# Two graph layers on a 4096-node adjacency: `adj` read in runs of 1 KB, eight groups of 32 rows a tile, from the second chunk on in two rounds of four tiles

## The chip, the cores and the metric

The kernel runs on one core of one Trainium2 chip. The metric is device time in microseconds. The kernel before took 587.05 us (median of 3 runs, 586.03 to 588.43).

## What is computed

Two graph layers over the same dense 4096 x 4096 float32 matrix `adj`. Shortened from the reference:

```
h  = relu(layernorm(x))
m  = mobius_matvec(weight, h); m = mobius_add(m, exp(bias)); x_tangent = logmap0(m)
support_t = adj @ x_tangent                      # 4096 x 4096 times 4096 x 128
x  = x + proj(expmap0(relu(logmap0(proj(expmap0(support_t))))))
h2 = relu(layernorm(x))
left, right = (context @ W_common.T) @ w_left + b_left, ... @ w_right + b_right
logits = leaky_relu(left[:, None] + right[None, :]), minus infinity where adj <= 0
x  = x + relu(softmax(logits) @ h2)
```

So `adj` (64 MB) is used once as numbers, in `adj @ x_tangent`, and once as a mask of edges, in the softmax.

## The kernel before

**Phase 1** reads `adj` once. TensorE contracts over partitions, so each piece of `adj` must be turned: nodes that are columns of `adj` have to lie on partitions. The 4096 rows are cut into 8 chunks of 512 rows (`NC = 8`, `CH = 512`), a chunk into 8 tiles of 512 columns (1 MB each), and a tile into 4 units, which the code calls blocks (`k`, 32 a chunk, `NK = 32`). `loaded` holds 4 tiles (`XSLOTS`), `turned` 4 units (`TSLOTS`). A tile comes in four loads of 256 KB, one for each 32 partitions (`b`): partitions 0 to 63 (`LOW`) are loaded by SP's queue, 64 to 127 (`HIGH`) by ACT's queue; the first four tiles all by SP's, and after them SP's queue brings `context` in 16 loads. A partition receives 16 runs of 128 floats, 512 B, from rows that lie 32 rows apart (line 281).

For each unit the engines do this, each in the order of its own program, coupled by semaphores:

- SP (line 360) waits until the last unit of a tile that held the slot is turned, then issues the slot's next two loads (line 362).
- DVE (`turn_block`, line 955) waits at a tile's first unit for its four loads (`adj_in`), at each unit for the product that used the `turned` slot (`block_multiplied`) and at every second for ACT's Sign (`half_signed`), and transposes 32 x 32 squares of a 128 x 512 piece (line 964).
- PE (`product`, line 678) multiplies `xt[:, k]` (128 x 128, float32) with the turned 128 x 512 piece and accumulates over the 32 units of the chunk into one of two banks, `acc[parity]` (line 686). Each float32 product stands in the profile as two records.
- ACT (`signs`, line 821) writes for each two units the sign of 1024 elements a partition into `mask`, int8, all of which stays in SBUF (line 836), and after every second Sign issues the two `HIGH` loads of the tile whose slot has come free (`load_high`, line 731). An issue that is held up holds up what ACT does after it.

After a chunk, ACT copies its sums (line 794, the first Sign of the next chunk stands before it), PE turns them (`turn_support`), and DVE, ACT and POOL do the norms and the residual beside the next chunk; POOL stores and loads rows of `x` (lines 561, 568).

In chunk 0, the tangent vectors `xt` are made on the fly: ACT makes a bias part for each of 32 blocks (`bias_part`, line 780, four ahead, then two after each Sign) and DVE makes a tangent from it (`tangent`, line 1081), one after each unit. PE's product of unit k waits for tangent k (`xt_ready`).

**Phase 2** (from about 325 us on) works from `mask` alone: comparisons, bit operations and products in fp8 and float16 (line 712). The order of nodes within a chunk is free as long as `x`, `context`, `out` and `adj` agree on it; lines 277 and 280 set it for the first three.

## Time and profile before

| | |
|---|---|
| median of 3 runs | 587.05 us (586.03 to 588.43) |
| span of the profiled execution | 587.9 us; no separate time of that one execution is given, and its span lies inside the three runs |
| instructions | 8561 |
| PE busy | 493.0 us, 84% |
| DVE busy | 448.0 us, 76% |
| ACT busy | 312.3 us, 53% |
| POOL busy | 268.5 us, 46% |
| DMA | 157445 packets, 84.72 MB, 144 GB/s over the span |

The span is one execution from the first to the last instruction. Busy shares are averages over two phases with different limits, so the page's 40 slices (of 14.7 us) come first, and then windows cut where a chunk ends. In "idle before" a number says how long an engine did nothing and what ended it. ACTq and SPq are the issuing of loads on these two queues; PEld is the weight load that belongs to a matmul.

### The profile page before, as it was taken

What the parts mean: (1) busy time and instruction counts of PE and PEld (TensorE: products, weight loads), DVE (VectorE), ACT (ScalarE), POOL (GpSimd) and SP (SyncE); (2) the same over time, 40 slices, a digit from 0 to 9 for tenths busy, and PEclk for the clock granted to TensorE, in tenths of its full rate; (3) what the DMA queues carried; (4) which work ended last, traced back from release to release, by engine and by line L of the source; (5) the groups of instructions that cost most, each with busy time, mean ns of one, the idle gap of its engine ahead of it and who ended that gap; (6) DMA issues with size and microseconds to landing.
All of it is one profiled execution on the core that took longest, in us unless ns stands there. A gap on an engine that the chain in (4) does not pass through costs nothing.

```text
span 587.9 us, 8561 instructions
## 1 busy us (share of the span) xinstructions
PE 493.0 (84%) x2695; PEld 309.4 (53%) x2695; DVE 448.0 (76%) x923; ACT 312.3 (53%) x466; POOL 268.5 (46%) x333
## 2 busy tenths in 40 slices
PE   2625999987989888888789457789999999999995
PEld 1522444332433332333333245668888888888884
DVE  4998987867767666656576999996969696969773
ACT  1666977655757556464465663243545444454521
POOL 5930057979696886917243799420202020111100
PEclk9976999999999999999899698989999999999998
DMA  7999999999999999999996010101010101011010
GB/s 161 218 222 213 233 287 284 288 265 266 247 274 277 236 258 240 251 234 228 216 250 146 19 37 1 37 18 37 19 37 21 37 19 37 19 37 37 1 37 18
DMA packets 157445, 84.72 MB, mean 144 GB/s; under 512 B 7600, under 2 KB 155312, under 8 KB 157408
## 3 DMA queue, kind: packets, MB, share of 16 engines
q1 hardware_dynamic: 89760, 47.60, 38.1%
q10 hardware_dynamic: 65232, 32.25, 26.2%
q0 software_dynamic: 2416, 4.41, 2.8%
q8 instruction: 19, 0.31, 0.2%
q14 instruction: 18, 0.15, 0.1%
HBM read 80.02 MB, written 4.21 MB: 143 GB/s over the span
## 4 chain that ended last, share of the span: by engine, by line
PE 36%; DMA 28%; DVE 20%; ACT 6%; issue 4%; ACTq 3%; POOL 2%; SPq 0%; DVEq 0%; POOLq 0%
PE ps L712 33%; DMA room<-in_adj_dram 27%; DVE room L964 5%; ACT mask L836 4%; PE ps L686 3%; ACTq L731 3%; DVE room L1199 2%; DVE room L1150 1%; DVE room L1166 1%; DVE mask L923 1%; DVE stats L1110 1%; DVE mask L976 1%; DVE room L1173 1%; DVE mask L972 1%; DMA mask<-in_x_dram 1%
## 5 line engine op out<-in xcount | busy, mean ns | idle before, releaser
L686 PE MATMUL ps<-room 128*128 128x512 f32 x512 | 241.5, 614 | 46.5 <-DVE room L964 29.0
L712 PE MATMUL ps<-room 128*128 128x258 f16 x2048 | 232.0, 276 | 23.2 <-POOL room L601 16.2
L712 PEld LDWEIGHTS ps<-room 128*128 128x128 fp8e4 x2048 | 200.4, 98 | 54.8 <-issue 16.9
L964 DVE STREAM_TRANSPOSE room<-room 128x512 f32<-128x512 f32 x256 | 167.0, 689 | 79.2 <-DMA room<-in_adj_dram 70.4
L836 ACT ACTIVATE mask<-room,constants 128x1024 int8<-128x1024 f32 x128 | 144.4, 1143 | 101.4 <-DVE room L964 92.9
L686 PEld LDWEIGHTS ps<-room 128*128 128x128 f32 x512 | 91.7, 192 | 190.8 <-DVE room L964 134.8
L615 POOL TENSOR_TENSOR h_room<-h_room 128x512 f32<-128x512 f32 x7 | 8.9, 1273 | 148.0 <-DVE post L1240 148.0
L1166 DVE SCALAR_TENSOR_TENSOR room<-mask,constants,room 128x512 int32<-128x512 int32 x64 | 62.2, 972 | 7.6 <-ACT room L885 7.6
L885 ACT ACTIVATE room<-relu_u,r_col 128x512 int8<-128x512 f32 x64 | 42.0, 713 | 42.3 <-PE ps L712 42.3
L885 ACT ACTIVATE room<-room,r_col 128x512 int8<-128x512 f32 x62 | 40.9, 712 | 34.1 <-PE ps L712 34.1
L464 POOL TENSOR_TENSOR mask<-mask,h_room 128x2048 f32<-128x2048 f32 x8 | 36.3, 4536 | 45.4 <-DVE room L1081 45.2
L1173 DVE SCALAR_TENSOR_TENSOR room<-mask,constants,room 128x512 int32<-128x512 int32 x64 | 47.6, 744 | 0.3
L473 POOL TENSOR_TENSOR mask<-mask 128x1024 f32<-128x1024 f32 (+6 forms) x56 | 44.9, 801 | 4.0
L1150 DVE TENSOR_SCALAR room<-room,r_col 128x512 int8<-128x512 f32 x66 | 37.6, 613 | 9.3 <-PE ps L712 9.3
L906 ACT ACTIVATE h_room<-ps,factors 128x258 f32<-128x258 f32 x32 | 15.2, 477 | 50.0 <-PE ps L712 49.0
L1150 DVE TENSOR_SCALAR room<-relu_u,r_col 128x512 int8<-128x512 f32 x64 | 32.2, 544 | 11.5 <-PE ps L712 11.5
L1229 DVE SCALAR_TENSOR_TENSOR h_room<-ps,factors,h_room 128x258 f32<-128x258 f32 x32 | 15.3, 485 | 16.8 <-ACT h_room L906 16.1
L568 POOL DMA_DIRECT2D xk<-in_x_dram x32 | 18.0, 569 | 19.4 <-ACT h_room L814 18.5
L532 POOL TENSOR_TENSOR post<-post,powers 128x8 f32<-128x8 f32 x8 | 13.5, 1686 | 24.6 <-DVE post L1104 24.6
L561 POOL DMA_DIRECT2D out_dram<-xk x32 | 18.3, 577 | 2.4 <-POOL xk L546 2.4
L1199 DVE SCALAR_TENSOR_TENSOR room<-h_room,factors,room 128x128 f16<-128x128 f32 x32 | 18.5, 639 | 0.0
L814 ACT ACTIVATE h_room<-xk,post 128x128 f32<-128x128 f32 x32 | 13.1, 479 | 9.8 <-POOL post L554 9.8
(158 smaller groups left out, 333.2 us busy)
## 6 DMA issues: line engine op xcount, KB each, us to landing
room<-in_adj_dram SPq DMA_DIRECT2D x136, 256.0 KB, 9.0
room<-in_adj_dram ACTq DMA_DIRECT2D x120, 256.0 KB, 10.9
mask<-in_L_gnn_context_dram SPq DMA_DIRECT2D x16, 256.0 KB, 10.8
xk<-in_x_dram POOLq DMA_DIRECT2D x32, 64.0 KB, 7.0
out_dram<-xk POOLq DMA_DIRECT2D x32, 64.0 KB, 6.5
h_room<-out_dram SPq DMA_DIRECT2D x32, 64.0 KB, 2.5
out_dram<-h_room SPq DMA_DIRECT2D x28, 64.0 KB, 1.7
mask<-in_x_dram SPq DMA_DIRECT2D x22, 64.0 KB, 4.2
```

The lines of the kernel that those rows point to most:

```text
L464: side(tt(room_of, cx[:, ks, :], v_rows[:, w, :].unsqueeze(1).broadcast_to([P, BESIDE, C]), ALU.mult))
L473: side(tt(dst, room_of[:, :, 0:n], room_of[:, :, n:2 * n], ALU.add))
L561: pool.dma_start(out_n[p, b], xk[b * Q:(b + 1) * Q]).then_inc(x1_stored, 16)
L686: pe.matmul(acc[parity], xt[:, k, :], turned[:, k % TSLOTS, :], start=(k == 0), stop=(k == NK - 1)).then_inc(block_multiplied, 1)
L712: mm = pe.matmul(ps[:, 2 * t + w, 0:GW], part[slot(c, g)][:, kk, t * P:(t + 1) * P], G[w][:, k, :], start=(k == 0), stop=(k == NK - 1))
L836: nc.scalar.activation(mc[:, half * HB:(half + 1) * HB, :], turned[:, slots:slots + HB, :], ACT.Sign, bias=constants[:, 4:5], scale=EDGE_S ...
L885: ins = nc.scalar.activation(signs_of[slot(c, g)][:, kk, :], nl[parity], ACT.Sign, scale=-1.0, bias=r_col[:, k:k + 1])
L964: v.transpose(turned[:, k % TSLOTS, :].rearrange("p (l b i) -> p b l i", l=L, b=NQ), loaded[:, g % XSLOTS, :, l * Q:(l + 1) * Q].rearrange ...
L1150: ins = v.tensor_scalar(signs_of[slot(c, g)][:, kk, :], nl[parity], r_col[:, k:k + 1], -1.0, ALU.is_gt, ALU.mult)
L1166: v.scalar_tensor_tensor(out=neg_words[n], in0=edges_of(c, g), scalar=ones, in1=neg_words[n], op0=ALU.bitwise_and, op1=ALU.bitwise_and).th ...
L1173: v.scalar_tensor_tensor(out=pos_words[n], in0=edges_of(c, g), scalar=ones, in1=neg_words[n], op0=ALU.bitwise_and, op1=ALU.bitwise_xor).th ...
L1199: v.scalar_tensor_tensor(out=G[1][:, k, D:2 * D], in0=h2[:, k, :], scalar=s1_col[:, k:k + 1], in1=G[1][:, k, 0:D], op0=ALU.mult, op1=ALU.s ...
```

## The change

Three things change together, and the names `W = 256` and `RH = 8` carry them.

1. **The shape of a tile.** A tile is now 256 rows by 1024 columns, the same 1 MB, still four loads of 256 KB for 32 partitions each. A partition receives 8 runs of 256 floats, 1 KB, from rows that lie 256 rows apart: eight groups of 32 rows a tile. A load has 256 runs where it had 512. The order of the nodes follows: a chunk's rows are eight groups of 32 rows in each half of the matrix, and `x`, `context` and `out` are addressed in the same order (`(l b s q)` for `(s b l q)`), still in runs of 512 B, 1 KB and 512 B.
2. **What a unit is.** A turned unit still is 128 x 512 elements, now two blocks of 128 columns of `adj` for 256 rows. PE makes two products with 256 columns each, with two blocks of `xt`, where it made one with 512; the sums of a chunk lie in the first 256 columns of two banks. ACT's Sign writes the same 1024 elements in four stretches of 256, the copy of the sums reads two stretches of 256.
3. **The order of tiles.** In chunk 0 the two row halves of a column group follow each other, so that half of the tiles need no new block of `xt`: DVE makes two tangents after each unit of an even tile and none in an odd one. From chunk 1 on the four column groups come for the first 256 rows and then for the next 256.

Late in phase 1 DVE waits for 24 instead of 16 products of the last chunk before it writes comparisons over `xt`.

```diff
+W = L * NQ * 16
+RH = L * NQ // 2
-        loaded = view(room, o, [XSLOTS, L * NQ, L * Q], F32)
+        loaded = view(room, o, [XSLOTS, RH, W], F32)
-        acc = [ps[:, 0, :], ps[:, 1, :]]
+        acc = [ps[:, 2 * n:2 * n + 2, 0:CH // 2] for n in (0, 1)]
-            return t.rearrange("(s b l q) d -> s b q l d", b=NQ, l=L, q=Q)
+            return t.rearrange("(l b s q) d -> s b q l d", b=NQ, l=L, q=Q)
-        cx_l = context.rearrange("(s b l q) d -> l b q s d", b=NQ, l=L, q=Q)
-        adj_n = adj.rearrange("(s r p) (g b j) -> s g b p r j", r=CH // Q, p=Q, b=NQ, j=L * Q)
+        cx_l = context.rearrange("(l b s q) d -> l b q s d", b=NQ, l=L, q=Q)
+        adj_n = adj.rearrange("(h r s q) (l b j) -> s l h b q r j", h=2, r=RH, q=Q, b=NQ, j=W)
+        def load_tile(eng, c, tile, quarters):
+            for b in quarters:
+                eng.dma_start(loaded[b * Q:(b + 1) * Q, tile % XSLOTS],
+                              adj_n[c, *run_and_half(c, tile), b]).then_inc(adj_in[tile % XSLOTS], 16)
+        def run_and_half(c, tile):
+            return (tile // 2, tile % 2) if isinstance(c, int) and c == 0 else (tile % L, tile // L)
+        def blocks_of(c, unit):
+            first = unit % L * 2 * L + run_and_half(c, unit // L)[0]
+            return first, first + L
+        tangent_order = [k for unit in range(NK) if unit // L % 2 == 0 for k in blocks_of(0, unit)]
...
                     if number and c == 0:
-                        pe.wait_ge(xt_ready, k + 1)
-                    pe.matmul(acc[parity], xt[:, k, :], turned[:, k % TSLOTS, :],
-                              start=(k == 0), stop=(k == NK - 1)).then_inc(block_multiplied, 1)
+                        pe.wait_ge(xt_ready, tangent_order.index(blocks_of(c, k)[1]) + 1)
+                    l, h = run_and_half(c, k // L)
+                    for j in range(2):
+                        mm = pe.matmul(acc[parity][:, h], xt[:, tangent_order.index(blocks_of(c, k)[j]), :],
+                                       turned[:, k % TSLOTS, j * (CH // 2):(j + 1) * (CH // 2)],
+                                       start=(l == 0 and k % L == 0 and j == 0),
+                                       stop=(l == L - 1 and k % L == L - 1 and j == 1))
+                    mm.then_inc(block_multiplied, 1)
...
-                    nc.scalar.activation(mc[:, half * HB:(half + 1) * HB, :], turned[:, slots:slots + HB, :],
+                    (l, h), s = run_and_half(c, half // HALVES), half % HALVES * L
+                    nc.scalar.activation(mc[:, l, h, s:s + L],
+                                         turned[:, slots:slots + HB, :].rearrange("p s (j i) -> p (s j) i", j=2),
                                          ACT.Sign, bias=constants[:, 4:5], scale=EDGE_SCALE).then_inc(
...
-                    turned[:, k % TSLOTS, :].rearrange("p (l b i) -> p b l i", l=L, b=NQ),
-                    loaded[:, g % XSLOTS, :, l * Q:(l + 1) * Q].rearrange("p (b l) q -> p b l q", b=NQ)).then_inc(
+                    turned[:, k % TSLOTS, :].rearrange("p (j r i) -> p j r i", j=2, r=RH),
+                    loaded[:, g % XSLOTS, :, 2 * l * Q:2 * (l + 1) * Q].rearrange("p r (j q) -> p j r q", j=2)).then_inc(
...
-                    if number and c == 0:
-                        tangent(k)
+                    if number and c == 0 and k // L % 2 == 0:
+                        for k_ in blocks_of(c, k):
+                            tangent(tangent_order.index(k_))
...
-            dve.wait_ge(block_multiplied, (NC - 1) * NK + NK // 2)
+            dve.wait_ge(block_multiplied, (NC - 1) * NK + NK - 2 * L)
```

How instructions stand in a row, DVE in chunk 0, units 8 to 12 (the transposes are line 964, the tangents 1081; in the changed kernel 985 and 1103). Before:

```order
L964 STREAM_TRANSPOSE room<-room 128x4x4x32 [waits half_signed,block_multiplied,adj_loaded_2]
L1081 SCALAR_TENSOR_TENSOR room<-mask 128x128 [waits fb_ready]
L964 STREAM_TRANSPOSE room<-room 128x4x4x32 [waits block_multiplied]
L1081 SCALAR_TENSOR_TENSOR room<-mask 128x128 [waits fb_ready]
L964 STREAM_TRANSPOSE room<-room 128x4x4x32 [waits half_signed,block_multiplied]
L1081 SCALAR_TENSOR_TENSOR room<-mask 128x128 [waits fb_ready]
L964 STREAM_TRANSPOSE room<-room 128x4x4x32 [waits block_multiplied]
L1081 SCALAR_TENSOR_TENSOR room<-mask 128x128 [waits fb_ready]
L964 STREAM_TRANSPOSE room<-room 128x4x4x32 [waits half_signed,block_multiplied,adj_loaded_3]
```

and now, from unit 7 to unit 13:

```order
L985 STREAM_TRANSPOSE room<-room 128x512 [waits block_multiplied]
L985 STREAM_TRANSPOSE room<-room 128x512 [waits half_signed,block_multiplied,adj_loaded_2]
L1103 SCALAR_TENSOR_TENSOR room<-mask 128x128 [waits fb_ready] x2
L985 STREAM_TRANSPOSE room<-room 128x512 [waits block_multiplied]
L1103 SCALAR_TENSOR_TENSOR room<-mask 128x128 [waits fb_ready] x2
L985 STREAM_TRANSPOSE room<-room 128x512 [waits half_signed,block_multiplied]
L1103 SCALAR_TENSOR_TENSOR room<-mask 128x128 [waits fb_ready] x2
L985 STREAM_TRANSPOSE room<-room 128x512 [waits block_multiplied]
L1103 SCALAR_TENSOR_TENSOR room<-mask 128x128 [waits fb_ready] x2
L985 STREAM_TRANSPOSE room<-room 128x512 [waits half_signed,block_multiplied,adj_loaded_3]
L985 STREAM_TRANSPOSE room<-room 128x512 [waits block_multiplied]
```

The tangents of units 12 to 15 have moved ahead, two behind each transpose of units 8 to 11, and from unit 12 on transposes follow each other directly.

ACT in chunk 0, units 4 to 7 (Sign, bias parts, the two loads of a tile's upper half). Before:

```order
L836 ACTIVATE mask<-room,constants 128x1024 [waits block_turned]
L780 ACTIVATE mask<-mask 128x128 [waits xt_ready] x2
L836 ACTIVATE mask<-room,constants 128x1024 [waits block_turned]
L780 ACTIVATE mask<-mask 128x128 [waits xt_ready] x2
L731 DMA room<-in_adj_dram 32x16x128 x2
```

and now:

```order
L856 ACTIVATE mask<-room,constants 128x4x256 [waits block_turned]
L798 ACTIVATE mask<-mask 128x128 [waits xt_ready] x2
L856 ACTIVATE mask<-room,constants 128x4x256 [waits block_turned]
L798 ACTIVATE mask<-mask 128x128 [waits xt_ready] x2
L288 DMA room<-in_adj_dram 32x8x256 x2
```

Nothing has moved here; the same two bias parts stand behind each Sign, and a load has 8 runs of 256 for each of 32 partitions instead of 16 of 128.

PE in chunks 0 and 1 (the products of `adj`, and `turn_support` between them). Before:

```order
L666 MATMUL ps<-mask 128x256 x2
L686 MATMUL ps<-room 128x512 x35
L675 MATMUL ps<-ident,room 128x128 x4
L686 MATMUL ps<-room 128x512 x29
```

and now:

```order
L683 MATMUL ps<-mask 128x256 x2
L705 MATMUL ps<-room 128x256 x70
L692 MATMUL ps<-ident,room 128x128 x4
L705 MATMUL ps<-room 128x256 x58
```

Each product of 512 columns has become two of 256; `turn_support` stands behind the same unit.

## Rows read from the trace of the kernel before

**Rows 1.** The page: 40 slices, busy tenths, granted clock, DMA, GB/s.

```profile
PE   2625999987989888888789457789999999999995
...
DMA  7999999999999999999996010101010101011010
GB/s 161 218 222 213 233 287 284 288 265 266 247 274 277 236 258 240 251 234 228 216 250 146 19 37 1 37 18 37 19 37 21 37 19 37 19 37 37 1 37 18
```

**Rows 2.** Windows: us, busy (x) of PE, PEld, DVE, ACT, POOL; PEclk, DMA, GB/s.

```profile
50.40:82.26 31.86, 31.79 (x69) 13.64 (x70) 27.67 (x63) 27.39 (x47) 2.64 (x1) 0.94 1.20 242
82.26:112.29 30.03, 29.17 (x68) 11.69 (x67) 23.79 (x46) 20.72 (x22) 25.78 (x28) 1.00 1.20 291
112.29:146.88 34.59, 29.70 (x68) 11.59 (x67) 25.42 (x46) 20.88 (x26) 29.73 (x36) 1.00 1.20 265
146.88:179.57 32.69, 30.57 (x71) 12.13 (x70) 24.02 (x47) 20.84 (x25) 26.78 (x37) 1.00 1.20 265
179.57:215.60 36.03, 30.94 (x71) 11.51 (x69) 24.17 (x46) 20.87 (x26) 28.71 (x30) 1.00 1.20 254
215.60:251.63 36.03, 31.36 (x70) 11.45 (x68) 23.36 (x46) 20.82 (x25) 26.32 (x39) 1.00 1.21 245
251.63:292.31 40.68, 31.28 (x67) 12.04 (x67) 23.83 (x49) 20.87 (x26) 15.40 (x27) 0.96 1.17 226
292.31:324.45 32.14, 29.21 (x65) 10.61 (x63) 22.09 (x46) 20.23 (x26) 14.24 (x28) 1.00 0.92 193
```

**Rows 3.** Chain of waits by line, 82 to 246, then 246 to 325 us.

```profile
by line: DMA room<-in_adj_dram 71.6%; DVE room L964 13.3%; ACT mask L836 3.8%; issue 3.5%; DVE stats L1110 2.0%; PE ps L686 2.0%; DVE post L1103 1.8%; DVE post L1099 1.8%; DVE post L1119 0.6%; DVE mv L1117 0.6%; ACTq L731 0.6%; DVE post L11
...
by line: DMA room<-in_adj_dram 37.2%; ACTq L731 19.4%; ACT mask L836 19.1%; PE ps L686 10.2%; DVE room L964 5.1%; issue 4.0%; ACT h_room L814 2.6%; DVE stats L1110 1.3%; ACT ps L801 0.6%; ACT ps L800 0.6%; DVE mv L1117 0.4%; DVE post L1119 
```

**Rows 4.** Who waited for line 362 (SP); line 731 (ACT): ns min/median/max, waits.

```profile
  DVE room L964: 1.1, 1
...
L731 ACTq DMA_DIRECT2D room<-in_adj_dram x120: 317/1768/5837, 51.1 to 307.3; - x120
...
  DVE room L964: 69.3, 48
```

**Rows 5.** DMA, one queue alone: 20 to 29, then 42 to 49 us.

```profile
DMA packets 3986, 1.99 MB, mean 221 GB/s; under 512 B 118, under 2 KB 3985, under 8 KB 3985
...
room<-in_adj_dram SPq DMA_DIRECT2D x8, 256.0 KB, 7.4
...
DMA packets 1582, 1.53 MB, mean 218 GB/s; under 512 B 92, under 2 KB 1582, under 8 KB 1582
...
mask<-in_L_gnn_context_dram SPq DMA_DIRECT2D x4, 256.0 KB, 10.8
```

**Rows 6.** DMA, both queues: 80 to 96, then 190 to 206 us.

```profile
DMA packets 9227, 4.62 MB, mean 289 GB/s; under 512 B 273, under 2 KB 9224, under 8 KB 9224
...
DMA packets 7260, 3.81 MB, mean 238 GB/s; under 512 B 283, under 2 KB 7195, under 8 KB 7259
```

**Rows 7.** Timeline of ACT, 283 to 294 us: an idle stretch for an issue.

```profile
282.94 1.15 ACT L836 ACTIVATE mask<-room,constants 128x1024 int8<-128x1024 f32 x1 [5.88 <-issue]
```

**Rows 8.** Groups of PE and PEld by form, and PE's timeline at 109 us.

```profile
L666 PE MATMUL ps<-mask 128*128 128x256 f32 x4 | 1.1, 405 | 0.0
...
L666 PEld LDWEIGHTS ps<-mask 128*128 128x128 f32 x4 | 0.7, 189 | 0.1
...
109.62 3.70 PE L686 MATMUL ps<-room 128*128 128x512 f32 x8 [0.55 <-DVE room L964]
113.16 0.60 PE L675 MATMUL ps<-ident,room 128*128 128x128 f32 x4
```

**Rows 9.** Timelines of ACT and of DVE in chunk 0.

```profile
53.27 0.68 ACT L780 ACTIVATE mask<-mask 128x128 f32<-128x128 f32 x2
...
59.33 0.31 DVE L1081 SCALAR_TENSOR_TENSOR room<-mask 128x128 f32<-128x128 f32 x1
59.56 0.70 DVE L964 STREAM_TRANSPOSE room<-room 128x512 f32<-128x512 f32 x1
```

More of the change, by code:

```diff
@@ L839, in signs @@
                     if number and c == 0:
[L840 to L841 removed]
+                        for n in range(XT_AHEAD + half * HB, min(NK, XT_AHEAD + (half + 1) * HB)):
+                            bias_part(n)
                     if half in steps:
```

40 lines of the change are left out of this document (18 added, 22 removed).

## The prediction

> **What bounds the kernel now.** I read the slices first. DMA stands at 9 tenths from slice 2 to slice 21, PE at 7 to 9 only from slice 5 on, and the moved GB/s are not constant: 284 to 288 in slices 6 to 8, 216 to 250 in slices 19 to 21 [rows 1]. So the first phase, up to about 325 us, is the part that loads `adj`, and the change touches nothing else of weight. Then I cut it at the eight copies of a finished chunk on ACT (line 794): the chunk passes take 31.9, 30.0, 34.6, 32.7, 36.0, 36.0, 40.7 and 32.1 us [rows 2]. The first two are PE's own pace, since PE is busy 31.79 of 31.86 and 29.17 of 30.03 us. In the later six PE idles 2 to 9 us a pass, and the loads run at 265 falling to 193 GB/s. The chain of waits says the same: from 82 to 246 us 71.6% of it is loads of `adj`; from 246 to 325 us it is 37.2% loads, 19.4% the issuing of loads on ACT's queue (line 731) and 19.1% ACT's Sign [rows 3]. And of the 70.4 us that DVE waits for tiles, 69.3 us are for loads that ACT issued, 1.1 us for SP's [rows 4]. ACT's issues have a median of 1.77 us and a longest of 5.84 us, where an unblocked one takes 0.32 us [rows 4], so the queue pushes back.
>
> What the queue pushes back with shows in the bytes. With one queue alone, packets of mostly 512 B ran at 221 GB/s and packets of mostly 1 KB (`context`) at 218 GB/s: 16 engines x 9 us / 3986 = 36.1 ns a packet of 499 B, and 16 x 7 / 1582 = 70.8 ns one of 967 B [rows 5]. There, time goes by bytes. With both queues level, 512 B packets reach 289 GB/s (16 x 16 us / 9227 = 27.7 ns each); later, with the same packets and the same two queues, 238 GB/s [rows 6].
>
> **The change part by part.** *Packets of 1 KB.* 131072 packets of 512 B become 65536 of 1 KB, same bytes. The lower bound of the gain is nothing, from the single-queue rows [rows 5]. The upper bound: if the part that goes by bytes is halved when both queues feed (36.1 / 2 = 18 ns) and the other 9.7 ns of the 27.7 are per packet, 1 KB takes 36 + 10 = 46 ns, or 356 GB/s, 20% over 289. The four passes from 112 to 252 us run at 245 to 265 GB/s, between both states, so I take the middle, 10%: 139.3 us (34.59 + 32.69 + 36.03 + 36.03) / 1.1 = 126.7, a gain of 12.7 us [rows 2]. The second pass is PE's: 32 blocks of 0.86 us and a turn_support of 0.60 us [rows 8] are about 28.5 us with the two handovers, so at most 1.5 us, and I take 0.9.
>
> *Issues.* With half the descriptors a queue holds more bytes before it pushes back: when SP went from loads of 512 descriptors to loads of 256 of the same 256 KB, the median from issue to landing went from 7.4 to 10.8 us at an unchanged 218 to 221 GB/s [rows 5]. So more lies queued, and ACT should issue in 0.3 to 0.5 us instead of 1.77. The pass of 40.68 us holds the longest idle stretch of ACT for an issue, 5.88 us [rows 7]. I let it fall to its neighbours' 36.03 / 1.1 = 32.8: 7.9 us. The last pass has PE idle 2.9 of 32.1 us; half of it, 1.5 us.
>
> *Matmuls.* A block's one product with 512 columns (two records of 0.43 us) becomes two with 256 columns, each with its own weights (eight records of 512 columns took 3.70 us). The nearest row has exactly the new shape: four records of 128x256 f32 in 1.1 us, 405 ns each with their overlap, so (1.1 - 0.4) / 3 = 0.23 us apart at most, the first one's longer start in it; the weight load lasts 0.19 us [rows 8]. Half of 0.43 is 0.215 us, and four such records are 0.86 us as before. I take 0; the bound above is 0.23 us a record, 0.06 us a block, 2 us a pass, which would fall on the passes that PE bounds. What hides a weight load is the preceding product of 0.215 us: it has 0.02 us to spare.
>
> *Transposes, signs, copies.* DVE's transposes read and write the same 128x512 (0.70 us), ACT's Sign the same 1024 elements (1.15 us), the copy the same 512 [rows 7, 9]. Only strides change. Either could rise by some tenths unseen: DVE is busy about 24 of 33 us a pass, ACT 21 [rows 2], so 0.1 us on each of 32 transposes would be covered. I take 0 for each, with bounds 0 and 1 us a pass.
>
> *Tangents.* In chunk 0 they come two with each unit of an even tile. ACT still makes two bias parts per Sign. In tiles 2, 4 and 6 the last pair must wait for the Sign of its own unit: a transpose 0.70, Sign 1.15, two bias parts 0.68, two tangents 0.54 (0.31, and 0.23 between two starts), so 3.1 us before PE has that block, where a block costs PE 0.86 [rows 7, 9]. Two units of such a tile wait; I get 10 us for a pair of tiles instead of 8 x 0.86 = 6.9, so up to 9 us for three pairs. Behind it on DVE stands the next transpose, and for that PE, ACT's Sign, and both queues' next loads, since a slot comes free later. Below, it costs nothing if loads bound the chunk anyway: four slots are a run-ahead of some 16 us of loading, and later passes wait for loads. I take 3 us.
>
> *The second phase.* DVE's wait for 24 instead of 16 blocks of the last chunk stands behind a transpose that needs 28, so it costs nothing. The loads of `x` and rows of `out` keep their 512 B.
>
> The sum, against the span of 587.9 us (the three timed runs have 586.0 to 588.4, median 587.05, so no correction): 587.9 - 12.7 - 0.9 - 7.9 - 1.5 + 3 = 567.9, and I say **568 us**.
>
> **A rule against the change.** In the rows above, eight groups of 32 rows a tile stand 32 rows x 16 KB = 512 KB apart before, and `context`'s runs too; no row shows a wider pitch. Afterwards the groups are 256 rows, 4 MB, apart. The Trainium skill, "DMA: Bandwidth & Descriptors", section "Latency and other measured facts", reports half the rate for a pitch of 4 MiB against one of 512 KiB (103 and 207 GB/s), where the streams of the partitions run in lockstep at that pitch. Here the 32 partitions of one load stay 16 KB apart and only an engine's successive packets lie 4 MB apart, so I hold it less likely than not; no run here shows it yet.
>
> A second rule explains the two rates: "SBUF — State Buffer", section "Door 1: The DMA port swizzle", says that partitions 0 to 63 reach only eight of 16 ports and gives 27.2 GB/s a port, 218 for eight. The rows agree (218 to 221 with one queue). By it packet size brings nothing whenever one queue leads.
>
> **The rivals.**
> *PE becomes the bound everywhere.* For: packets were fast once the queues were level, 291 GB/s in the second pass, and only 8.9 MB a pass are needed, 312 GB/s at PE's 28.5 us. Then 82.3 + 3 + 7 x 28.5 = 284.8 where 324.4 stands: 39.6 less, 548 us; with the whole 9 us of tangents 554. Against: it needs 7% more than the best stretch, sustained.
> *Bytes, not packets.* The rate stays as it is and only ACT's stall goes, which the tangents eat: 587.9 - 0 to 5 + 3, about 588 us. For: rows 5. Against: rows 6, where 512 B packets take 27.7 ns.
> *The wider stride slows the loads.* Mechanism: successive packets of an engine, 4 MB apart, meet the same part of the memory and queue there. Place: every load of `adj`. From 82 to 324 us 59.9 MB are moved, on average 247 GB/s; that is the point from which it decides. At the 220 GB/s of rows 5 it is 272 us instead of 242: 588 + 30 + 3 = 621 us; at 240 GB/s, 599.
> *Tangents uncovered with no gain in rate*: 587.9 + 9 - 1.5 = 595 us.
>
> **How the numbers follow.** Forecast as summed (556 to 582): 0.45. PE as the bound (546 to 556): 0.20. Bytes (584 to 590): 0.12. Wider stride: 0.15. Tangents alone: 0.08. A change of 0.5% is about what a measurement of this kernel can tell from none. So faster 0.65, same 0.12, slower 0.23. The range of 8 in 10 runs from the PE bound to the mild form of the stride: 547 to 600; it leaves the severe stride and the lower edge outside.
>
> **What would show it.** DMA slices should read 265 GB/s or more from 82 us on with about 65,000 fewer packets; the median of ACT's issues of `adj` below 1 us; DVE's wait for loads well under 70 us; PE's records twice as many with the same total of busy time; passes 3 to 7 of about 31 us; the first pass 3 to 9 us longer, with DVE or PE waiting on bias parts. I am wrong if the GB/s of passes 2 to 6 are at or below 247, if weight loads leave PE idle between two products of a block, or if the passes stay long while DMA drops below 9 tenths.

## The result and the profile after

The changed kernel takes 572.51 us (median of four runs, 570.08 to 573.64); the kernel before takes 587.74 us beside it (four runs, 586.03 to 589.52). The ratio is 0.9725, with a 95% interval of 0.9679 to 0.9771. The forecast was 568 us in a range of 547 to 600. A second series, on another chip, gave 573.08 us (571.16 to 574.06) for the changed kernel and 583.1 us for the kernel before (median of eleven runs, 578.32 to 600.02), with a ratio of 0.9853 (0.9789 to 0.9917). So the changed kernel repeats its time within 0.6 us, the kernel before does not, and the gain is 15.2 us in the first series and 8 to 10 us in the second. (All ratios leave out executions that fell in the chip's slower state; of one experiment below, the kernel before with an addition moved, that leaves one of four, so it carries no verdict.)

The profiled run of after took 573.64 us with a span of 571.8 us against 587.9, so 16.1 us have to be placed. No trace shows a run of before near 580 us; how much of each difference below is such scatter of before, and how much the change, is not shown.

The first phase can be cut at the same eight copies of a finished chunk as in [rows 2]; they are at line 812 now. The view is the windows of after, with the columns of [rows 2]: us, busy time (and instructions) of PE, PEld, DVE, ACT, POOL; PE's granted clock, DMA share, GB/s.

```profile
50.70:90.32 39.62, 33.93 (x130) 27.49 (x131) 28.70 (x62) 26.97 (x45) 5.85 (x2) 0.88 0.95 211
90.32:120.25 29.93, 29.30 (x138) 25.50 (x137) 26.49 (x47) 21.05 (x22) 22.20 (x26) 1.00 1.08 282
120.25:153.04 32.79, 28.41 (x128) 24.41 (x128) 27.96 (x47) 21.23 (x25) 30.11 (x37) 0.94 0.96 276
153.04:184.22 31.18, 30.70 (x138) 26.44 (x137) 26.44 (x47) 21.31 (x26) 24.45 (x30) 0.96 1.02 282
184.22:217.46 33.24, 28.86 (x128) 24.24 (x128) 27.74 (x47) 21.09 (x26) 30.06 (x37) 0.94 0.96 273
217.46:248.86 31.40, 30.91 (x138) 26.59 (x137) 26.45 (x47) 21.31 (x26) 24.45 (x30) 0.95 1.03 282
248.86:280.64 31.78, 28.59 (x131) 24.75 (x131) 24.68 (x49) 21.20 (x25) 17.91 (x35) 0.97 1.10 257
280.64:310.94 30.30, 28.67 (x130) 24.07 (x128) 23.19 (x49) 20.12 (x26) 14.66 (x29) 0.98 0.84 226
310.94:571.84 260.90, 231.70 (x2052) 200.44 (x2052) 211.55 (x362) 114.99 (x209) 70.84 (x64) 0.97 0.10 26
```

Against [rows 2], pass by pass: the first is 7.8 us longer (39.62 for 31.86) and starts 0.3 us later. The second is level (29.93 for 30.03). The third to sixth take 128.6 us for 139.3, which is 10.7 less. The seventh takes 31.78 for 40.68, 8.9 less, the eighth 30.30 for 32.14, 1.8 less. What follows the last copy takes 260.9 us; before it took 587.9 - 324.45 = 263.4, so 2.5 less. 8.1 - 0.1 - 10.7 - 8.9 - 1.8 - 2.5 = -15.9, which is the difference of the spans but for rounding. The change does not touch the second phase. 260.8 us stand there in several experiments too, and 261.0 in another trace of the kernel before (the experiment with its addition moved), so the profile of before was a little long in that part; I have no cause for it.

The page of after, the lines that answer to [rows 1], and its count of packets:

```profile
PE   1724879999699979999697648799999999999995
...
DMA  7999899999799998999893010101111010101010
GB/s 165 201 230 226 198 226 233 281 285 324 221 268 305 292 311 199 299 284 300 221 286 91 21 37 1 38 20 38 22 36 29 29 32 25 39 18 38 1 38 18
DMA packets 91911, 84.75 MB, mean 148 GB/s; under 512 B 7600, under 2 KB 89776, under 8 KB 91872
```

There are 65,534 packets fewer than the 157,445 of before. The rate is no longer falling from pass to pass: 282, 276, 282, 273, 282 GB/s stand where [rows 2] had 291, 265, 265, 254, 245. But DMA drops to 7 or 8 tenths every few slices, and PE's digit falls to 6 or 7 in the same slice or beside it. So something other than loads now interrupts the work. Who waits is told by the line that issues the loads (288), which answers to [rows 4]. Columns: ns min/median/max, first and last start; then who waited for the loads, us and times.

```profile
L288 SPq DMA_DIRECT2D room<-in_adj_dram x136: 311/452/1414, 13.8 to 296.0; - x136
L288 ACTq DMA_DIRECT2D room<-in_adj_dram x120: 318/415/1735, 51.1 to 296.1; - x120
...
  DVE room L985: 12.0, 10
```

ACT's issues have a median of 0.415 us instead of 1.768 (all 120 together 56.4 us instead of 191.0), and DVE waits 12.0 us for loads instead of 70.4. The chain of waits from 90 to 248 us, which answers to the first line of [rows 3], has turned from loads to PE:

```profile
by line: PE ps L705 54.5%; DMA room<-in_adj_dram 12.7%; issue 9.6%; DVE room L985 9.3%; POOL mask L490 3.6%; DVE stats L1132 2.4%; PE ps L692 1.1%; POOL post L549 1.1%; DVE mv L1139 1.0%; POOL xk L563 0.8%; POOL relu_u L561 0.7%; POOL post 
```

### The profile page after: what moved, and what is told of

The parts are those of the page before. It is cut to its first block, busy times and chain, and to the rows that moved or that the text cites. A ratio compares the mean times of both kernels' runs of the same rounds, so it can differ in the third digit from the quotient of the medians.

```text
span 571.8 us, 9585 instructions
## 1 busy us (share of the span) xinstructions
PE 488.3 (85%) x3207; PEld 419.0 (73%) x3207; DVE 463.6 (81%) x923; ACT 314.1 (55%) x466; POOL 267.7 (47%) x333
## 4 chain that ended last, share of the span: by engine, by line
PE 56%; DVE 20%; DMA 8%; issue 5%; POOL 5%; ACT 4%; ACTq 1%; DVEq 0%; POOLq 0%
PE ps L734 34%; PE ps L705 21%; DVE room L985 5%; DMA room<-in_adj_dram 4%; DMA top_right<-h_room 2%; DVE room L1222 2%; ACT mask L856 2%; DVE room L1173 1%; DMA h_room<-top_right 1%; DVE room L1189 1%; POOL mask L490 1%; DVE mask L944 1%; POOL post L549 1%; DVE mask L997 1%; DVE room L1196 1%
## 5 line engine op out<-in xcount | busy, mean ns | idle before, releaser
L705 PE MATMUL ps<-room 128*128 128x256 f32 x1024 | 237.5, 393 | 38.1 <-DVE room L1103 23.0
L705 PEld LDWEIGHTS ps<-room 128*128 128x128 f32 x1024 | 200.3, 198 | 73.3 <-DVE room L985 37.2
L985 DVE STREAM_TRANSPOSE room<-room 128x512 f32<-128x512 f32 x256 | 172.1, 696 | 35.7 <-PE ps L705 16.8
L856 ACT ACTIVATE mask<-room,constants 128x1024 int8<-128x1024 f32 x128 | 146.2, 1145 | 85.5 <-DVE room L985 84.0
L927 ACT ACTIVATE h_room<-ps,factors 128x258 f32<-128x258 f32 x32 | 15.2, 476 | 49.4 <-PE ps L734 48.4
```

Of the source, the lines that this page charges most:

```text
L705: mm = pe.matmul(acc[parity][:, h], xt[:, tangent_order.index(blocks_of(c, k)[j]), :], turned[:, k % TSLOTS, j * (CH // 2):(j + 1) * (CH / ...
L856: nc.scalar.activation(mc[:, l, h, s:s + L], turned[:, slots:slots + HB, :].rearrange("p s (j i) -> p (s j) i", j=2), ACT.Sign, bias=const ...
L985: v.transpose(turned[:, k % TSLOTS, :].rearrange("p (j r i) -> p j r i", j=2, r=RH), loaded[:, g % XSLOTS, :, 2 * l * Q:2 * (l + 1) * Q].r ...
```

## Experiments

Each kernel below is the changed kernel with one edit, unless the text says otherwise. Passes are counted as the rows above are; where an expectation speaks of the sixth pass it starts counting behind the first copy, and means the seventh row.

### The tangents of chunk 0

The first pass of after is 7.8 us longer than before. Its stalls inside the pass show who waits. The view is the timeline of DVE in after; the brackets give idle time and what ended it.

```profile
64.41 0.64 DVE L1103 SCALAR_TENSOR_TENSOR room<-mask 128x128 f32<-128x128 f32 x2 [1.51 <-ACT mask L798]
...
71.02 0.64 DVE L1103 SCALAR_TENSOR_TENSOR room<-mask 128x128 f32<-128x128 f32 x2 [0.35 <-ACT mask L798]
...
73.80 0.64 DVE L1103 SCALAR_TENSOR_TENSOR room<-mask 128x128 f32<-128x128 f32 x2 [1.51 <-ACT mask L798]
...
80.41 0.64 DVE L1103 SCALAR_TENSOR_TENSOR room<-mask 128x128 f32<-128x128 f32 x2 [0.35 <-ACT mask L798]
...
83.19 0.65 DVE L1103 SCALAR_TENSOR_TENSOR room<-mask 128x128 f32<-128x128 f32 x2 [1.51 <-ACT mask L798]
```

The waits of after from 50 to 90 us: who waited for whom, us in all, times, longest.

```profile
PE ps L705 <- DVE room L1103: 23.0, 6, 17.3
...
DVE room L1103 <- ACT mask L798: 7.6, 8, 1.5
```

In three tiles (2, 4 and 6) DVE stands 1.51 us for ACT's bias part, after a stall of 0.35 to 0.39 us two units earlier; behind DVE stands the next transpose, and PE has no block meanwhile. Of the 23.0 us that PE waited for tangents, 17.3 are the start of the phase. The other 5.7 fall in the pass, and the granted clock of the pass is 0.88 instead of 0.94, so that PE's busy time rises from 31.79 to 33.93 us: 5.7 + 2.1 = 7.8 us. The second part varies: in the second series' trace of the same kernel this pass has a clock of 0.93, PE busy 31.67 us, and its copy stands at 88.32 us instead of 90.32. The stalls are undone by giving ACT eight slots for bias parts instead of four:

```diff
-XT_AHEAD = 4
+XT_AHEAD = 8
```

> The changed kernel with eight bias parts ahead on ACT instead of four (XT_AHEAD = 8), nothing else. Theory: the first chunk got 8 us longer (copy at 90.3 instead of 82.3 us) because DVE's tangents wait in tiles 2, 4 and 6 for bias parts that stand behind the Sign of their own unit (7.6 us of waits, line 1103 for 798), and with it PE; eight ahead take these waits away. Then the first copy comes back to about 84 us, and since the loads now run faster than PE needs them, all later passes keep their lengths: 566 to 568 us, 5 to 7 less than the 572.5 of the changed kernel. Rival: loads bound the passes behind it anyway, and the time won in chunk 0 is waited for later: within 1 us of 572.5, with DVE's wait for adj (12 us) up by as much.

564.38 us (563.8 to 568.2, four runs), ratio to before 0.9693 (0.9589 to 0.9798; the runs of before scattered on this chip). That is 2 us below the expected range, since the first copy comes at 80.8 us and not at 84. The windows of this kernel, first and second pass:

```profile
50.50:80.77 30.27, 30.07 (x130) 25.85 (x131) 27.69 (x63) 27.13 (x47) 4.37 (x1) 0.94 1.07 257
80.77:110.59 29.82, 29.20 (x137) 25.41 (x137) 26.38 (x47) 21.04 (x23) 23.68 (x27) 1.00 1.08 310
```

The first pass is 30.27 us, shorter than before's own 31.86. The other passes are unchanged to 0.3 us up to the sixth. So the tangents cost 8 to 9 us of the new kernel, by medians of different chips (572.51 and 573.08 against 564.38; the changed kernel was not run on this one).

### The wait of a small DVE instruction for POOL

From the third pass on, passes of 33 and of 31 us alternate, PE idles 4.4 us in the long ones, and DMA's share falls to 0.96. The place is found on the timelines of DVE and of POOL in after, at 145 us:

```profile
145.60 4.55 DVE L1141 TENSOR_SCALAR post<-mv 128x4 f32<-128x4 f32 x1
150.07 1.88 DVE L985 STREAM_TRANSPOSE room<-room 128x512 f32<-128x512 f32 x3
```

POOL at the same time:

```profile
145.60 4.51 POOL L481 TENSOR_TENSOR mask<-mask,h_room 128x2048 f32<-128x2048 f32 x1
```

The addition of epsilon to four variances, 128x4 elements, lasts 4.55 us. It has the duration of POOL's 4.51 us product that starts with it; alone it takes 0.17 us. While it lasts no transpose runs, and PE uses up its four blocks. PE's timeline at the same time:

```profile
150.82 5.44 PE L705 MATMUL ps<-room 128*128 128x256 f32 x13 [4.38 <-DVE room L985]
```

Two windows behind the stall, with the columns of [rows 2]:

```profile
150.80:154.00 3.20, 3.18 (x8) 2.55 (x9) 2.57 (x4) 3.10 (x4) 3.12 (x3) 0.50 0.44 70
158.00:160.00 2.00, 2.00 (x11) 1.74 (x11) 1.76 (x3) 2.00 (x5) 0.17 (x1) 1.00 1.04 298
```

Behind the stall the granted clock is 0.50, and eight records take 3.18 us where eleven take 2.00 us later, at 1.00.

In the first five passes behind the first copy this instruction lasts 1.90, 4.55, 1.75, 4.56 and 1.76 us, together 14.5; in the trace of before the same line (1119 there) has 0.72, 2.37, 0.47, 0.98 and 0.17, together 4.7. The second of these, from the timeline of DVE in before:

```profile
141.62 2.37 DVE L1119 TENSOR_SCALAR post<-mv 128x4 f32<-128x4 f32 x1
```

POOL's product beside it:

```profile
139.42 4.53 POOL L464 TENSOR_TENSOR mask<-mask,h_room 128x2048 f32<-128x2048 f32 x1
```

The two end within 0.04 us of each other, as the two that start at 145.60 us in after do. In both traces every one of these additions in phase 1 that lasts over 0.4 us starts while a POOL TENSOR_TENSOR runs and ends 0.03 to 0.04 us behind it. So the hold was there before; what is new is when the addition starts: 2.2 and 3.6 us into POOL's two long products in before, together with them in after. The longer hold comes from the timing of two engines, which the change moved without touching either instruction. The Trainium skill, "SBUF — State Buffer", section "Who interferes with whom", says that a DVE instruction of this kind and a POOL operation can take turns on a shared pair of ports for the whole of an instruction. The trace agrees in the common ends; that ports are what is shared is not shown by a run. What the instruction costs on DVE is shown by the experiment, in which the addition is POOL's own:

```diff
-                    chain(ins)
-                    v.tensor_scalar(post[:, 40:44], mv[:, :, 1], LN_EPS, None, ALU.add).then_inc(var_ready, 1)
+                    ins.then_inc(var_ready, 1)
...
+                chain(nc.gpsimd.tensor_scalar(post[:, 40:44], mv[:, :, 1], LN_EPS, None, ALU.add))
```

(The counts of steps on both engines, POST and POOL_POST, go from 3 to 2 and from 7 to 8.)

> The changed kernel, in which POOL and not DVE adds epsilon to the variances: the 128x4 TENSOR_SCALAR of line 1141 leaves DVE. Theory: that instruction takes 4.55 us in two passes and 1.8 to 1.9 us in three others (14.5 us in all, 4.7 us before the change) because it starts while POOL runs a TENSOR_TENSOR on SBUF, and DVE's transposes, PE and the next loads stand behind it; without it the passes of 32.8 and 33.2 us fall to about 29.5 and those of 31.2 to 31.4 to 29.5: 562 to 566 us. Rival: the wait is not on the path, since DVE has 12 us of waits for loads and PE's clock is down for other reasons: 570 to 573 us.

562.65 us (561.03 to 566.05, five runs), ratio 0.9629 (0.9537 to 0.9721). That is in the expected range. Its windows, third and fourth pass:

```profile
115.94:146.28 30.34, 29.83 (x138) 25.25 (x137) 23.86 (x46) 21.31 (x25) 27.79 (x37) 1.00 1.09 312
146.28:175.40 29.12, 28.94 (x133) 24.26 (x133) 23.47 (x46) 21.16 (x26) 26.95 (x32) 1.00 1.07 293
```

Both passes have PE busy to within 0.6 us of their length, the granted clock is 1.00 where it was 0.94 and 0.96, and the loads run at 312 and 293 GB/s, more than in any pass of after. The second to sixth pass take 147.6 us instead of 158.5. So about 10 us of what the faster loads bring were given back here. Moving a small instruction off DVE, with the loads as they were, released them.

Whether the same wait costs anything in the kernel before was asked with the same edit in it:

> The kernel before, with the addition of epsilon to the variances moved from DVE to POOL, and nothing else. Theory: in the changed kernel this small DVE instruction is held by a long POOL operation (1.8 to 4.6 us a pass, 14.5 us over the first five), in the kernel before only for 4.7 us, most of it in passes whose end is set by late loads. So moving it is worth little here: 0 to 3 us of 583, that is 580 to 583, while it was worth 10 us in the changed kernel. Rival: the hold costs the same in both, or the move helps for another reason (a shorter DVE stream); then it gives 5 to 10 us here too, 573 to 578.

The one execution to go by took 581.04 us; the three runs of before beside it that can be compared took 574.24, 578.63 and 580.28. That fits "worth little" and excludes little. This stays open; what the two traces show is only that the instruction lasted 4.7 us in all in before, in passes in which DVE waited 70 us for loads.

### Packets of 512 B in the new arrangement

The loads are halved; the count for which DVE waits is doubled with them.

```diff
-                eng.dma_start(loaded[b * Q:(b + 1) * Q, tile % XSLOTS],
-                              adj_n[c, *run_and_half(c, tile), b]).then_inc(adj_in[tile % XSLOTS], 16)
+                for v in (slice(0, W // 2), slice(W // 2, W)):
+                    eng.dma_start(loaded[b * Q:(b + 1) * Q, tile % XSLOTS, :, v],
+                                  adj_n[c, *run_and_half(c, tile), b][:, :, v]).then_inc(adj_in[tile % XSLOTS], 16)
```

> The changed kernel with every load of adj as two loads of half as many bytes, left and right half of each run: packets of 512 B in 512 loads of 128 KB, same rows, same pitch of 4 MB, same bytes. Theory of packets: 512 B packets take at least 27.7 ns each, so passes 1 to 5 go at 289 GB/s at best and 240 to 265 on average, passes of 33 to 36 us, and ACT's issues of adj take twice the time; with the longer chunk 0 that is 588 to 598 us. Rival, bytes alone: the gain came from the order of tiles or from the other pitch, and 570 to 575 us stand.

585.04 us (579.47 to 588.74, ten runs), ratio 1.0086 (1.0035 to 1.0138). With 512 B packets the gain is gone, as expected of packets, though the time is 3 us below the expected range. But the way is not the one I had assumed. The chain of waits of this kernel, 90 to 248 us, and the line of its loads:

```profile
by line: ACTq L289 23.9%; ACT mask L857 23.0%; DVE room L986 16.1%; issue 10.8%; PE ps L706 7.1%; POOL mask L491 3.6%; ACT h_room L834 2.6%; DVE stats L1133 2.3%; DVE post L1126 1.1%; DVE post L1122 1.1%; POOL post L550 1.1%; DVE mv L1140 1
```

ACT's issues of loads (ns min/median/max), and who waited for loads:

```profile
L289 ACTq DMA_DIRECT2D room<-in_adj_dram x240: 347/532/4931, 51.2 to 301.8; - x120
...
  DVE room L986: 7.3, 4
```

Almost nothing waits for a load (7.3 us). ACT waits while it issues, up to 4.9 us at a time and 161.7 us in all (191.0 in before, 56.4 in after), and the Signs behind those issues come late: "ACTq" and "ACT mask" are 47% of the chain. So a large part of what the smaller packets cost comes through the queue's push-back on ACT, whose work stands behind the issues. The rate falls as well, to 267 to 269 GB/s in passes three to six (273 to 282 in after); the two parts are not separated. This kernel is not the kernel before: it has twice as many issues, and DVE waits for loads 7.3 us in it and 70.4 in before, with packets of the same size. What of the gain belongs to the number of packets and what to the order and size of the loads, the experiment doesn't separate.

### Halves of the partitions, and queues

The Trainium skill, "SBUF — State Buffer", section "Door 1: The DMA port swizzle", which the prediction draws on, says that partitions 0 to 63 reach only eight of 16 ports. In the changed kernel SP loads the quarters 0 and 1, ACT 2 and 3. Here SP takes 0 and 2, ACT 1 and 3, so that both work on the same half at a time:

```diff
-load_tile(sp, c, g, (0, 2, 1, 3) if first_tiles else LOW)
+load_tile(sp, c, g, (0, 2, 1, 3) if first_tiles else (0, 2))
...
-load_tile(act, c, tile, HIGH)
+load_tile(act, c, tile, (1, 3))
```

> The changed kernel with the quarters of a tile dealt otherwise from the fifth tile on: SP's queue loads quarters 0 and 2, ACT's 1 and 3, so that both queues fill partitions 0 to 63 at the same time and then both 64 to 127. Theory of two halves: 230 GB/s is what one half of the partitions takes, so with both queues in step the loads of adj stay near 220 to 240 GB/s, passes of 37 to 40 us: 605 to 630 us. If the queues drift apart by one load, they are on different halves again and it is nearer 580. Rival: the partitions don't matter, only packets and queues: 570 to 575 us.

612.73 us (605.17 to 613.67, five runs), ratio 1.0501 (1.0399 to 1.0603). Then all loads on SP's queue:

```diff
-load_tile(sp, c, g, (0, 2, 1, 3) if first_tiles else LOW)
+load_tile(sp, c, g, (0, 2, 1, 3) if first_tiles else range(NQ))
...
-load_tile(act, c, tile, HIGH)
+pass
```

> The changed kernel with all loads of adj on SP's queue, in the order of the quarters 0, 1, 2, 3, and none on ACT's; every load, packet and slot as before. Theory A (a load of one quarter runs at the 220 to 232 GB/s that the lone queue showed, and only two queues on different halves of the partitions overlap): the passes run at 220 to 235 GB/s, 38 to 40 us each, about 610 to 620 us in all, like the run with both queues on one half at a time (612.7). Theory B (a deep queue keeps two or more loads in flight, so one queue with alternating quarters is as good as two): 265 to 290 GB/s and 573 to 580 us. ACT's idle time for issues goes away in both.

625.72 us (625.11 and 626.33), ratio 1.0831 (1.069 to 1.0972). The middle passes are 39.2 to 39.5 us, as the first theory has it. In all it is 6 us beyond its range, but the range was summed too low: a first copy at 90.4 us, seven passes of 38 to 40 us and a second phase of 261 us make 617 to 631. The packets of three kernels in the same stretch, 120 to 152 us, from the view of DMA; first after:

```profile
DMA packets 9037, 9.01 MB, mean 282 GB/s; under 512 B 654, under 2 KB 8906, under 8 KB 9034
```

Both queues on one half at a time:

```profile
DMA packets 7491, 7.38 MB, mean 230 GB/s; under 512 B 496, under 2 KB 7425, under 8 KB 7489
```

One queue:

```profile
DMA packets 7281, 7.23 MB, mean 226 GB/s; under 512 B 519, under 2 KB 7186, under 8 KB 7279
```

The same 1 KB packets move at 230 and 226 GB/s where two queues work on different halves at 282 GB/s, which is not even the limit: the window holds the 4.4 us in which the work stands still. In other passes of the kernel with both queues on one half it is 234 to 254 GB/s; whether its queues stay in step is not shown. Two queues that fill the same half are little or no better than one. Here the traces agree roughly with the rule on ports (the Trainium skill gives 218 GB/s for eight of them), not with the reading that packet size decides everything.

### The pitch of 4 MB

Row groups 32 rows apart (512 KB), all else as in the changed kernel. This kernel reads each byte once, but the sums it makes are for other nodes, so it doesn't compute the reference:

```diff
-        adj_n = adj.rearrange("(h r s q) (l b j) -> s l h b q r j", h=2, r=RH, q=Q, b=NQ, j=W)
+        adj_n = adj.rearrange("(s h r q) (l b j) -> s l h b q r j", h=2, r=RH, q=Q, b=NQ, j=W)
```

> The changed kernel with the eight groups of 32 rows of a tile taken 32 rows apart instead of 256, so a pitch of 512 KB as before and not 4 MB; it reads other rows than it should, each byte once, and its sums are for other nodes. Same packets of 1 KB, same work. Theory: the pitch costs nothing, because the 32 partitions of a load lie 16 KB apart in both: within 2 us of the unedited changed kernel. Rival: the wide pitch slows the loads (half the rate at 4 MB in the Trainium skill, DMA: Bandwidth & Descriptors): then this one is faster, passes 3 to 7 nearer 28 to 30 us, 560 to 566 us, and more bytes a microsecond while both queues are full than the 284 GB/s of the changed kernel.

570.41 us (568.64 to 570.98, four runs), ratio 0.9804. The changed kernel once more, on the same chip and in the same rounds:

> The changed kernel itself, unedited, so that the others of this chip have it beside them. 570 to 575 us.

573.08 us, ratio 0.9853 (0.9789 to 0.9917). The 2.7 us between the two are a little more than the 2 us expected, and the runs do not overlap. In the traces the narrow pitch is 4.8 us shorter in the seventh pass (29.70 for 34.52) and longer by 1.8 and 1.5 in the first and the eighth. The second to sixth take 158.2 and 159.2 us, so the pitch costs at most 1 us there; a small cost in all is not excluded. The seventh pass of the unedited kernel took 31.78 us in the first series. Why it is long is the next question.

### A store of 4 B from each partition

The seventh pass is the longest or second longest in eleven of the thirteen traces of kernels that have the store of this section (not in that of after), and in it the loads come to a near halt. The moved GB/s of after from 260 to 282 us, in slices of 0.55 us, from the view of DMA:

```profile
GB/s 276 240 296 345 350 341 352 330 307 345 346 343 339 352 353 357 349 345 177 69 86 101 127 91 91 71 32 28 82 130 207 307 307 250 330 376 384 386 367 233
```

POOL's timeline in after, with what it issues there:

```profile
262.38 2.10 POOL L501 DMA_DIRECT2D neg_left<-h_room  x4 [0.29 <-POOL post L552]
264.47 0.58 POOL L503 DMA_DIRECT2D top_right<-h_room  x1
...
268.40 2.26 POOL L578 DMA_DIRECT2D out_dram<-xk  x4 [0.30 <-POOL xk L563]
277.37 0.59 POOL L507 DMA_DIRECT2D h_room<-top_right  x1 [6.71 <-DMA top_right<-h_room]
```

The halt begins at about 270 us and ends before 277, when the row is read back; so it is neither the read nor its copies. POOL's store of 512 B, 4 B from each of 128 partitions, is issued at 264.47 and lands 12.6 us later, and a wait for it is 20% of the chain of waits from 248 to 311 us. The expectations below call it 128 packets of 4 B; the trace's DMA records have 16 packets of 32 B, which start at 268.77 to 268.95 us, about 1 us before the halt. The kernel before has the same store, issued at 270.97 us, and a shallower dip behind it. Its GB/s from 268 to 286 us, in slices of 0.45 us:

```profile
GB/s 215 257 209 247 222 216 259 213 244 233 216 256 217 230 245 217 260 229 239 248 208 230 217 143 135 150 120 126 110 139 165 183 168 193 209 228 297 343 327 349
```

From 278.4 to 282 us it moves 110 to 165 GB/s. The 16 packets of 32 B start there at 275.43 to 277.00 us. For this question I took the fastest version, with both repairs above and one more: the maximum over the row that is read back is taken at block 8 of the last chunk instead of block 3, so that DVE no longer waits for that row (4.4 us in after, 5.9 with the two repairs). First the two repairs together, then the third:

```diff
-XT_AHEAD = 4
+XT_AHEAD = 8
...
-                    v.tensor_scalar(post[:, 40:44], mv[:, :, 1], LN_EPS, None, ALU.add).then_inc(var_ready, 1)
...
+                chain(nc.gpsimd.tensor_scalar(post[:, 40:44], mv[:, :, 1], LN_EPS, None, ALU.add))
```

> The changed kernel with both earlier edits: eight bias parts ahead, and epsilon added on POOL. Theory: the two stalls lie in different passes (chunk 0; the ends of passes 1 to 5) and nothing stands behind them but PE's own pace, so the gains add: chunk 0 back to 81 us and passes 1 to 5 of 28 to 31 us, 553 to 557 us. Rival: once both are gone the loads bound, since a pass needs 8.9 MB and 28 us asks for 318 GB/s; then passes 1 to 5 are 31 us again and it is 560 to 563 us, with DVE's waits for loads over 20 us.

555.32 us (553.78 to 558.55, six runs), ratio 0.9555 (0.9504 to 0.9605). The two gains add: the single edits were 8.7 and 10.4 us below the 573.1 of the changed kernel, which gives 554.0 (the single edits ran on another chip than the 573.1).

```diff
-                    steps[7] = exponentials
+                    steps[8] = exponentials
...
-                    if c == NC - 1 and k == 3:
+                    if c == NC - 1 and k == 8:
```

> As the kernel with both edits, and in the last chunk DVE takes the largest right score after unit 8 instead of unit 3 and ACT the exponentials after its 9th Sign instead of its 8th. Theory: DVE stands up to 4 us at unit 3 for a transfer (top_row) that lands late; later there is no wait: 1 to 4 us below the kernel with both edits. Rival: the loads of adj are themselves held up in that stretch (one wait of DVE of 6.5 us at the end of the pass before), so DVE is late there anyway and nothing is gained: within 1 us.

553.35 us (552.45 to 554.2, six runs), ratio 0.9516 (0.9471 to 0.956): the fastest version that computes the reference, though 2 us below the one ahead of it are hardly more than the spread of the two. Against it stands the same kernel in which the 4-byte store is left out and another row is read back; the number that keeps the exponents small is then not the largest:

```diff
-                pool.wait_ge(top_ready, 1)
-                pool.dma_start(top_dram, extreme[:, 0:1]).then_inc(top_stored, 16)
...
-                pool.wait_ge(top_stored, 16)
-                pool.dma_start(top_row, top_dram.rearrange("p a -> a p").broadcast_to([P, P])).then_inc(top_loaded, 16)
+                pool.wait_ge(nl_stored, 16 * NQ)
+                pool.dma_start(top_row, nl_dram[0:1].broadcast_to([P, P])).then_inc(top_loaded, 16)
```

> The best version so far (eight bias parts ahead, epsilon on POOL, later maximum) without the store of the 128 per-partition maxima as 128 packets of 4 B: the row that is read back comes from the first row of neg_left instead, so the number that keeps the exponents small is not the largest of r; the rest of the work is the same. Theory: the 4-byte store, or the read behind it, holds the 16 DMA engines, which fall below 130 GB/s for some 3 to 4 us in the sixth pass; without it the sixth pass goes from 32.7 us to about 29.5 to 30.5 and the time from 553.4 to 550 to 552. Rival: the dip is from something else (four stores of neg_left, the loads' own order, x and out rows on POOL's queue); then pass and time stay at 32.7 and 553.

> The best version so far once more, unchanged, beside the run without the 4-byte store, so that both traces are from one chip. By either theory: 552 to 555 us, a sixth pass of 32 to 33.5 us with a dip of the loads in it.

549.69 us (549.68 and 549.7) without the store, 554.83 (551.86 and 557.8) with it, on one chip, two runs each. Both passes lie outside what was expected: without the store 28.88 us for 29.5 to 30.5, with it 34.69 for 32 to 33.5. The window of the seventh pass with the store:

```profile
229.32:264.01 34.69, 29.14 (x131) 24.58 (x131) 24.10 (x48) 21.15 (x25) 20.75 (x40) 0.96 1.13 259
```

The same pass without it:

```profile
228.65:257.53 28.88, 27.62 (x129) 23.67 (x129) 23.67 (x48) 21.15 (x26) 20.19 (x39) 1.00 1.10 303
```

The GB/s from 248 to 262 us, in slices of 0.35 us, with the store:

```profile
GB/s 269 304 342 337 328 323 301 337 348 372 349 347 354 331 258 26 26 29 23 26 29 35 41 47 47 50 176 269 290 243 243 240 231 225 237 287 211 222 366 383
```

The same stretch without it, with its count of packets:

```profile
GB/s 313 325 301 338 282 321 349 349 358 357 342 281 331 354 345 348 348 339 418 287 424 401 363 354 386 369 331 354 348 348 340 334 293 298 337 348 345 348 339 342
DMA packets 4901, 4.79 MB, mean 342 GB/s; under 512 B 479, under 2 KB 4821, under 8 KB 4901
```

With the store the rate falls to 23 to 50 GB/s for 4 us and then stays near 240; without it nothing falls below 281, and the pass is 5.8 us shorter. The fall begins at 252.9 us, 1 us behind the store's 16 packets of 32 B (251.82 to 251.94). The four stores of `neg_left` and the rows of `out` on POOL's queue stay in both kernels, so the halt is not theirs. So the store costs this kernel 4 to 5 us, by the medians of 553.35 and 554.83 against 549.69, and 2 to 8 us by the single runs of this chip. By what mechanism 512 bytes hold 16 engines is not shown.

## Why the prediction held, point by point

*What bounds the kernel*: as said. Loads bound passes three to seven of before; with faster loads DVE's wait for them goes from 70.4 to 12.0 us.

*Packets of 1 KB, 12.7 us*: 10.7 us came, and the two agree by accident. The rate itself gained more than the 10% that I took. Where nothing breaks the stream, in the kernel without the small store, 4901 packets of 977 B on average in 14 us are 16 x 14 / 4901 = 45.7 ns each, 342 GB/s. That is near the upper bound of the prediction, 46 ns for a full 1 KB and 356 GB/s (which is 23% over 289, not 20%). Without the wait for POOL the four passes take 30.3 + 29.1 + 30.9 + 29.3 = 119.6 us, 19.7 below before. Of these 9.0 were given back by the small addition on DVE. The step that failed is the line "only strides change" on DVE: I priced the edits, and not the DVE instructions that stay. Before, DVE waited 6 to 17 us a pass for loads from the second pass on, and the hold lasted at most 2.4 us; in after it lasts up to 4.56 us and DVE waits at most 4.6 us a pass. That such a hold would have been hidden in before is likely, but no run shows it.

*The second pass, 0.9 us*: 0.1. It is PE's in both, but the addition holds DVE 1.90 us in it; with that moved it takes 27.96 us, 2.1 less than before.

*Issues, 7.9 us*: the pass of 40.68 us came down by 8.9, and the median of ACT's issues is 0.415 us, inside the 0.3 to 0.5 forecast. The reason I gave, that more bytes lie queued, is not what the trace shows: ACT's loads land 7.8 us behind their issue instead of 10.9 at about the same or a higher rate, so not more is under way. And the stall itself may have a second cause. The 5.88 us stall of [rows 7] runs from 277.06 to 282.94 us, over the dip behind the 4-byte store of before (issued at 270.97). The changed kernel has the halt too, and a deeper one. How the 8.9 us divide between push-back and halt is not shown.

*The last pass, 1.5 us*: 1.8.

*Matmuls, 0*: right. Two products of 256 columns cost what one of 512 did, and the bound of 0.06 us a block stayed unused. The line of the products in after:

```profile
L705 PE MATMUL ps<-room x1024: 379/379/796, 50.7 to 310.5; 128*128 128x256 f32 x171
```

PE's timeline in after, to compare with the eight records of 3.70 us in [rows 8]:

```profile
99.76 17.64 PE L705 MATMUL ps<-room 128*128 128x256 f32 x81
118.03 3.72 PE L705 MATMUL ps<-room 128*128 128x256 f32 x16 [0.62 <-DVE room L985]
```

16 records in 3.72 us are four blocks, as eight in 3.70 us were, and 81 records run in 17.64 us, 0.218 us apart, with no gap for a weight load.

*Tangents, +3 of 0 to 9*: 8.1, near the upper bound (6.1 by the trace of the second series). The mechanism was right to the instruction (the last pair of an even tile waits for its Sign and bias parts); the cover that I trusted wasn't there. I had written that it costs nothing if loads bound the chunk anyway, but [rows 2] has PE busy 31.79 of 31.86 us in this very pass. A bound beside a busy PE should have been taken at its upper end: 587.9 - 12.7 - 0.9 - 7.9 - 1.5 + 9 = 573.9, which is the measured time within 1.5 us. Even so errors cancel in it: the loads' gain is put 2.8 us too high, that of the last two passes 1.3 too low, the tangents' cost 0.9 too high, and the 2.5 us of the second phase are not in it.

*The rivals*: "Bytes, not packets" falls with the rate (282 and up to 342 GB/s) and with the run of 512 B packets at 585 us, though not by the way that I had in mind. The stride, as a loss of half the rate, falls with the pitch run (at most 2.7 us): the Trainium skill, "DMA: Bandwidth & Descriptors", section "Latency and other measured facts", has half the rate where the partitions of a copy are 4 MiB apart, but in this kernel's loads, where the partitions of one load are 16 KB apart and the row groups 4 MB, the trace doesn't show it (273 to 282 GB/s a pass, and 339 to 357 in the slices of after from 266 to 270 us, all at 4 MB). PE as the bound everywhere is what the repaired kernels reach: 548 us was the rival's time, 553.35 and, without the small store, 549.69 were measured.

## What to carry to other kernels

Faster loads uncover what the wait for loads had hidden: before such a change, list the long instructions of the engine that waited, among them short ones that last as long as a neighbour's, and price each as if no load were late. A bound whose cover is a busy engine is taken at its upper end. In this kernel it paid to give each queue its own half of the partitions, to load in packets of 1 KB instead of 512 B, and to look for a store of single words beside the stream of loads.

## What of the hardware was not expected

- Four numbers a partition on DVE (128x4) last 4.55 us beside a POOL product of 4.51 us, 2.37 us when they start 2.2 us into one of 4.53, and 0.17 us alone.
- Two queues that fill the same half of the partitions move 230 GB/s (up to 254 in other passes), one queue 226; on different halves 282 and, unbroken, 342 GB/s.
- Behind a store of 4 B from each of 128 partitions (16 packets of 32 B) the 16 engines fall to 23 to 50 GB/s for 4 us, some 5.5 us after its issue and 1 us after its packets start; it lands 12.6 to 12.8 us after its issue.
- In a pass in which PE stands idle 4.4 us the granted clock is 0.94, in the same pass without the stall 1.00. Products last 379 ns at a granted clock of 1.00 and up to 796 ns, about twice as long, where it is 0.50 (2.4 and 1.2 GHz), so a stall costs more than its length.
